# The first chunk of a feed-forward net is normalized beside the last unit of attention

## The reference

```python
x = _layernorm(x + attention(x))          # x is (1, 4096, 256), 16 heads of 16, rotary q and k
x = _layernorm(x + ffn(x))

def ffn(x):                               # 256 -> 1024 -> 1024 -> 1024 -> 256
    h = silu(tlin(x, w1_w, w1_s)) * tlin(x, w2_w, w2_s)
    h = gelu(tlin(h, h1_w, h1_s))         # tlin(x, w, s) = (x @ w.T) * s
    h = gelu(tlin(h, h2_w, h2_s))
    return tlin(h, w3_w, w3_s)
```

## Time and profile before

| | |
|---|---|
| Median of 3 runs | 3526.78 us (3524.37 to 3530.44) |
| Profiled execution, its own time | 3524.76 us |
| Its span (first to last instruction) | 3523.1 us |
| Mean granted clock of TensorE, 1 being full | 0.971 |
| PE busy | 3384.9 us (96%) |
| DVE busy | 2987.0 us (85%) |
| ACT busy | 2451.1 us (70%) |
| POOL busy | 184.7 us (5%) |

### The profile page before, as it was taken

The page is one execution under the profiler, slowest core; times in us unless marked ns, Lnnn a source line. Parts: engine busy times, 40 slices in busy tenths (PEclk is TensorE's granted clock), DMA queues, the critical chain, the costliest instruction groups (busy, mean ns, idle before and its releaser), DMA issues. The chain is left out here.

```text
span 3523.1 us, 67331 instructions
## 1 busy us (share of the span) xinstructions
PE 3384.9 (96%) x27994; PEld 1536.3 (44%) x27994; DVE 2987.0 (85%) x3188; ACT 2451.1 (70%) x4472; POOL 184.7 (5%) x320
## 2 busy tenths in 40 slices
PE   8569999999999999999999999999999699999998
PEld 3223333333333333333333333333333278888887
DVE  6599999999999999999999999999996045555554
ACT  2108888888888888888888888888889622222222
POOL 3300000000000000000000000000000000000000
PEclk9759999999999999999999999999999899999999
DMA  8920000000000010001000000000000220000000
GB/s 212 219 42 6 20 12 12 24 12 12 12 24 16 15 60 14 12 11 61 11 12 30 14 12 12 12 12 12 12 8 5 92 96 25 25 25 26 25 13 13
DMA packets 60037, 113.78 MB, mean 32 GB/s; under 512 B 11719, under 2 KB 23624, under 8 KB 59560
## 3 DMA queue, kind: packets, MB, share of 16 engines
q1 hardware_dynamic: 53048, 93.83, 9.7%
q0 software_dynamic: 6688, 15.68, 1.5%
HBM read 82.20 MB, written 37.22 MB: 34 GB/s over the span
## 5 line engine op out<-in xcount | busy, mean ns | idle before, releaser
L710 DVE TENSOR_REDUCE group_max<-wide 128x2 f32<-128x1024 f32 x2048 | 2473.0, 1223 | 22.5 <-PE wide L521 15.8
L681 ACT ACTIVATE probs<-scores 128x512 f32<-128x512 f32 x4046 | 2202.9, 600 | 290.1 <-PE scores L606 42.0
L547 PE MATMUL sums<-probs,v_all 128*17 128x256 f32 (+1 forms) x16120 | 1277.2, 389 | 7.7 <-ACT mixed L664 6.8
L606 PE MATMUL scores<-q_sb,k_all 51*128 51x512 f32 x3968 | 988.5, 495 | 6.7 <-ACT probs L681 5.7
L521 PE MATMUL wide<-k_all,q_sb 48*128 48x512 f32 x4096 | 850.1, 411 | 52.9 <-DVE group_max L710 26.7
L606 PEld LDWEIGHTS scores<-q_sb,k_all 51*128 51x128 f32 x3968 | 370.6, 183 | 842.9 <-ACT probs L681 829.4
L547 PEld LDWEIGHTS sums<-probs,v_all 128*17 128x17 f32 x16120 | 267.1, 95 | 747.4 <-issue 364.9
L521 PEld LDWEIGHTS wide<-k_all,q_sb 48*128 48x128 f32 x4096 | 397.6, 190 | 91.5 <-DVE group_max L710 63.9
L1073 ACT ACTIVATE whole_hid<-acc,scale 128x512 f32<-128x512 f32 x128 | 84.7, 689 | 297.5 <-PE acc L954 297.3
L954 PE MATMUL acc<-hid_b,h2T 128*128 128x512 f32 x1024 | 241.6, 397 | 0.0
L954 PE MATMUL acc<-hid_a,h1T 128*128 128x512 f32 x1024 | 240.2, 394 | 0.0
(11 more groups left out here) (88 smaller groups left out, 1171.1 us busy)
## 6 DMA issues: line engine op xcount, KB each, us to landing
k_all<-k_parts SPq DMA_DIRECT2D x96, 128.0 KB, 5.2
q_sb<-q_parts SPq DMA_DIRECT2D x192, 64.0 KB, 2.5
q_parts<-parts SPq DMA_DIRECT2D x16, 512.0 KB, 6.0
k_parts<-parts SPq DMA_DIRECT2D x16, 512.0 KB, 6.3
heads<-mixed SPq DMA_DIRECT2D x128, 34.0 KB
xt<-in_xT SPq DMA_DIRECT2D x8, 512.0 KB, 6.3
w_words<-in_h1T POOLq DMA_DIRECT2D x32, 128.0 KB, 2.4
w_words<-in_h2T POOLq DMA_DIRECT2D x32, 128.0 KB, 2.3
```

The costliest lines, as they stand in the source:

```text
L547: last = pe.matmul(sums[32 * j:32 * j + HD + 1, cols], v_all[:, g, kt, j], probs[(kt * HG + j) % RING][:, cols], start=(kt == 0 and cols.s ...
L606: pe.matmul(scores[(s + e) % BANKS][:], k_all[rows, g * GP + j, n // HG * P:(n // HG + 1) * P], q_sb[g][rows, j], start=True, stop=True).t ...
L681: act.activation(probs[n % RING][:], bank, ACT.Exp, scale=INV_SCALE)\
L710: dve.reduce_max(group_max[:, n], wide[n % 2][:], AX_X).then_inc(wide_free, 1)
```

## The change

`attend` now also computes the front of chunk 0. A new class `FirstChunk` lays its tiles, and those of w1T, w2T and h1T, over the place of `k_all` for groups 0 and 1 (what is loaded) and group 2 (x1, x1t, statistics). SP issues the loads after the stores of unit 29 (`load_first`), and the exchange of the inverted sums ahead of the stores of unit 30 (`share_first`). PE has fixed places for its part in the last unit (`beside_last`), where the unread pair of products stands otherwise; ACT takes the square root ahead of the first tile of step 18; DVE does its part after its last maxima. SP no longer waits for the last unit's stores at the block's end: they count on `last_stored`, for which SP and POOL wait in `feed_forward`. There SP first issues h2T and w3T, then the loads of chunk 1; DVE adds, with nine more counts, to the semaphores what the front of chunk 0 would have added, and PE begins with the flag, the branch and `gate_layer(0)`.

```diff
+EARLY_W = ("w1T", "w2T", "h1T")
+            def load_first():
+                for p in range(2):
+                    sp.wait_ge(mixed_free[p], 16 * HG * 3)
+                load_sums(sp, heads_dram, fc.inverse_sums, 0, sums0_in)
+                load_heads(sp, heads_dram, fc.heads, 0, heads0_in)
+                sp.dma_start(fc.x[:], chunk_of(io["x"], 0)).then_inc(x0_in, 16)
+                sp.dma_start(fc.wo[:], io["woT"].rearrange("(f p) o -> p f o", p=P)).then_inc(small0_in, 16)
...
+                sp.wait_ge(w_copied, 16 * len(W_AT))
+                for name in EARLY_W:
+                    load_weights(sp, w_dram, fc.w[name], name, w0_in)
+            def share_first():
+                sp.wait_ge(inverted0, 1)
+                store_inverse(sp, shares_dram, fc.inverse_sums, 0, inverse0_out)
+                sp.wait_ge(inverse0_out, 16)
+                for f in range(FT):
+                    load_shares(sp, shares_dram, fc.shares, 0, f, shares0_in[f])
             for g in range(NG):
                 if g < NG - 1:
                     place_shift((NCH - 1) * NG + g + 1, g + 1)
-                finish(NCH - 1, g)
+                if g == NG - 2:
+                    share_first()
+                finish(NCH - 1, g, mixed_free[g % 2] if g < NG - 1 else last_stored)
+                if g == 1:
+                    load_first()
             for p in range(2):
-                sp.wait_ge(mixed_free[p], 16 * HG * (1 + UNITS // 2))
-            sp.wait_ge(w_copied, 16 * len(W_AT))
+                sp.wait_ge(mixed_free[p], 16 * HG * (1 + UNITS // 2 - p))
+            sp.wait_ge(w0_in, 16 * len(EARLY_W))
+            sp.wait_ge(small0_in, 16 * SMALL)
...
+        BITS_AT, TOK_AT, ROOT_AT, FLIP_AT, SPLIT_BY = 4, 10, 18, 21, 26
+            def beside_last(g, kt):
+                if kt == BITS_AT:
+                    pe.wait_ge(low_done, 1)
+                    pe.wait_ge(ident_set, 3)
+                    pe.matmul(wide[1][0:1, 0, 0:1], low_bits[:], ones[:], start=True, stop=True).then_inc(bits0_summed, 1)
+                elif TOK_AT <= kt < TOK_AT + TT:
+                    tok_first(kt - TOK_AT)
+                elif FLIP_AT <= kt < FLIP_AT + FT:
+                    flip_first(kt - FLIP_AT)
+                elif kt < BITS_AT or BITS_AT + 3 <= kt < TOK_AT:
+                    if kt == BITS_AT + 3:
+                        pe.wait_ge(flag0_set, 1)
+                    unread_pair(g)
+                elif ROOT_AT - 1 <= kt < FLIP_AT:
+                    pe.wait_ge(norm0, TT)
+                    unread_pair(g)
+                elif kt >= SPLIT_BY:
+                    pe.wait_ge(x1t0_step, 2 * FT)
+                    unread_pair(g)
...
+                    if last and n == ROOT_AT * HG:
+                        act.wait_ge(norm0, 3 * TT + 1)
+                        act.activation(fc.root[:], fc.spread[:], ACT.Sqrt).then_inc(root0_done, 1)
...
+            for name in w_in:
+                load_weights(sp, w_dram, w_sb[name], name, w_in[name])
+            load_chunk(1)
+            sp.wait_ge(last_stored, 16 * HG)
...
-            pe.wait_ge(ident_set, 3)
-            pe.matmul(flip[0][0:1, 0:1], low_bits[:], ones[:], start=True, stop=True).then_inc(bits_summed, 1)
-            pe.wait_ge(small_in, 16 * SMALL)
-            front(0)
-            pe.wait_ge(flag_set, 1)
-            front_flip(0, 0)
             low = pe.value_load(flag[0:1, 0:1], min_val=0, max_val=1)
...
-            act.wait_ge(small_in, 16 * SMALL)
-            front_root(0)
             gates(0)
...
+            dve.sem_inc(divided, FT)
+            dve.sem_inc(inverted, 1)
...
+            dve.sem_inc(x1t_step, 2 * FT)
             gates(0)
```

More of the change, by code:

```diff
@@ L358, in attend @@
         probs = [sb(f"probs{r}", [P, CH]) for r in range(RING)]
-        mixed = [sb(f"mixed{p}", [P, CH]) for p in range(2)]
-        ident = sb("ident", [P, P])
+        ones = sb("ones", [P, 1])
         group_max = sb("group_max", [P, MAXG, PAIR])
@@ L570, in last_unit @@
                         if j == 0:
[L572 to L575, removed]
+                            beside_last(g, kt)
                     if kt > 0:
@@ new lines, in _ @@
+            dve.tensor_scalar(fc.flag[:, 0:1], wide[1][0:1, 0, 0:1], 1.0, None, ALU.min).then_inc(flag0_set, 1)
+            dve.wait_ge(heads0_in, FT * 16)
+            for f in range(FT):
+                dve.wait_ge(shares0_in[f], 16)
+                dve.tensor_tensor(fc.heads[:, f], fc.heads[:, f], fc.shares[f][:], ALU.mult).then_inc(divided0, 1)
+            dve.wait_ge(x0_in, 16)
+            for t in range(TT):
+                if t % 2 == 0:
+                    dve.wait_ge(tok0_ready, t // 2 + 1)
+                dve.tensor_tensor(fc.x1[:, t], tok[t // 2][:, t % 2], fc.x[:, t], ALU.add).then_inc(norm0, 1)
@@ new lines, in _ @@
+            for t in range(TT):
+                dve.wait_ge(norm0, t + 1)
+                dve.bn_stats(fc.stats[:, t], fc.x1[:, t]).then_inc(norm0, 1)
+            for t in range(TT):
+                dve.wait_ge(norm0, TT + t + 1)
+                dve.sem_inc(waited0, 1)
+                dve.bn_aggr(fc.moments[:, t], fc.stats[:, t]).then_inc(norm0, 1)
+            dve.wait_ge(norm0, 3 * TT)
+            dve.tensor_scalar(fc.spread[:], fc.moments[:, :, 1], EPS, None, ALU.add).then_inc(norm0, 1)
@@ L754, in sem @@
             return ctx.enter_context(nc.semaphore(name))
[L756 to L770, removed]
-        hid_a = [sb(f"hid_a{h}", [P, HT, CH], F32R) for h in range(2)]
+        fc = first_chunk
+        hid_a = [sb(f"hid_a{h}", [P, HT, CH], F32R) for h in range(2)]
+        sb("before_first_chunk", [P, (fc.at - nc.sbuf_base) // 4])
+        sb("first_chunk", [P, (fc.end - fc.at) // 4])
+        wo, heads, shares, inverse_sums, x_sb, x1t = fc.wo, fc.heads, fc.shares, fc.inverse_sums, fc.x, fc.x1t
+        scale, scale3, flag = fc.scale, fc.scale3, fc.flag
+        w_sb = dict(fc.w)
+        for name, (_, rows, cols) in W_AT.items():
+            if name not in w_sb:
+                w_sb[name] = sb(name, [P, rows // P, cols])
+        x1 = [fc.x1, sb("x1_1", [P, TT, D])]
         hid_b = [sb(f"hid_b{h}", [P, HT, CH], F32R) for h in range(2)]
@@ L817, in feed_forward, with load_chunk @@
         HIDS = 3 * HT
-        SUM_COLS = H * CH // P
-        HF = H // FT
         NORM1 = 4 * TT + 2
         NORM2 = 5 * TT + 2
-        SMALL = 1 + 4 + 1
         EARLY = 3
         block = ctx.enter_context(nc.Block())
[L829 to L841, removed]
         @block.sync
         def _(sp):
[L845 to L850, removed]
+            def load_chunk(c):
+                load_heads(sp, heads_dram, heads, c, heads_in)
+                sp.dma_start(x_sb[:], chunk_of(io["x"], c)).then_inc(x_in, 16)
             def store(c):
@@ L1026, in step @@
                         gate_layer(c + 1)
-                for name in ("w1T", "w2T"):
-                    pe.wait_ge(w_in[name], 16)
                 gate_layer(0)
-                for name in ("h1T", "h2T", "w3T"):
+                for name in w_in:
                     pe.wait_ge(w_in[name], 16)
```

206 lines of the change are left out of this document (142 added, 64 removed).

## The result

The changed kernel takes 3484.08 us, median of 4 runs (3482.10 to 3487.24), beside 3526.82 us (3524.37 to 3530.44) for the kernel before: a ratio of 0.9885, 95% interval 0.9872 to 0.9897. That is 42.7 us less. Forecast were 31.3 us less, 3495.5, range 3489 to 3504. In two experiments one execution each (4910 and 3940 us) is left out of the numbers as disturbed.

The account below looks back on a forecast made before the run. VectorE bounds most of attention, untouched; ACT paces the last unit, and the passage is a chain with nothing beside it. Terms: -31.8 - 6.6 + 2.9 + 1.0 + 2.0 + 1.6 - 0.4 + 0 = -31.3 us, median 3495.5, range 3489 to 3504.

Parts of the forecast that it names:

- (a): Passage: the front of chunk 0, from the net's start to the first gate product, goes; 31.8 us less.
- (b): Passage: SP's wait for the last stores at the block's end goes; 6.6 us less.
- (g): Net's start: eleven semaphore counts on DVE, then PE's flag and branch; 1.6 us more, up to 3.9.
- (c): Last unit, ACT: two table loads, the square root and overlap lost once; 2.9 us more.
- (e): Last unit: PE's clock falls once after idling during the table loads; 2.0 us more, bounds 0 and 3.1.
- (d): Last unit, PE steps 10 to 13: products with wo replace unread pairs, partly absorbed by PE's lead; 1.0 us more.
- (f): Last unit: PE's fixed slots never wait for their producers; 0 us.
- (h): First gate layer: a slightly less slow start after shorter idling; 0.4 us less than the present 17.8.
- (i): First hidden layer: h2T and w3T land at most 18.2 us after the net's start, before needed; 0 us.
- Rival 1: Block's end: the barrier still waits for the last stores through outstanding DMAs; 3502 us, chance 0.08.
- Rivals 2 and 4: Last unit: clock falls several times, 3502 us, chance 0.10; or falls at step 5 and stays low, 3540, chance 0.02.
- Rival 3: Net's start: two late weights come later than a gate layer, branch could need 2.3 more; 3498 to 3501, chance 0.06.

Follow-up runs that it names:

- after_mix2: Changed kernel with x1t, hid_a and hid_b moved 128, 1024 and 512 bytes further from their weights (modulo 2048); 3485.56 us, one execution.
- after_tok8: Changed kernel with its eight products with wo one to a step over steps 7 to 14, not two over 10 to 13; 3489.12 us.
- after_best: Changed kernel with the inverse root on DVE and PE's wait for h2T and w3T after the first hidden layer; 3477.61 us.
- before_free_end: Kernel before with only the wait for the last stores moved out of the block's end into the net; 3520.64 us beside 3525.95.
- before_nopair: Kernel before with the unread pair of products left out of all 32 steps of the last unit; 3520.93 us, one execution.
- after_best2: As after_best, with all unread pairs of the last unit left out too; 3476.39 us, median of three.

## Why the prediction was wrong

By its own steps:

- **The parts behind the first gate layer** were costed at nothing, silently. The steps priced every instruction moved, added or removed, and took those left alone to keep their durations. That is the step that failed: the diff gives the net's tiles other places in SBUF, the distance of moving operand and weights went from -64 to 0 bytes, and the 2496 wide products behind the first gate layer got 16.2 us shorter together (6.7 ns each in the hidden layers, start to start); the eight layers with w3T, where w3T is the moving operand and went from +64 to +256 of hid_a, take 7.92 us instead of 7.78 and give 1.1 back. The stretch as a whole is 15.2 us shorter, and the same got from the kernel before by a pad alone. Without it the result would be about 3484.1 + 15.2 = 3499, inside the range and above the forecast of 3495.5 by the other misses below. The trace before could hardly show it, since all products there went at one pace; a look at the places would have raised the question, but not given the sign.
- **(a), (b), (g)**, the passage: -37.1 against -36.8. Right, and PE takes the branch within the 1.3 us from SP's first issue to its own first product. The upper bound of 3.9 us for a branch that stalls did not come.
- **(c)** 3.1 against 2.9, right. **(e)** one fall behind one gap, as forecast, at 1.2 us against 2.0. But "expect the clock to fall once" is no certainty: it did not in after_mix2, and cost 2.6 in after_tok8.
- **(d)** right in that PE is late in its four steps, wrong in the lead and in the size: 4.2 us net (4.7, less 0.5) against 1.0. Four parts were off: a step of PE without its slot takes 1.84 us and not 1.58 (1.0 us over four steps), the two products hold PE for 1.06 and not 0.86 (0.8), the lead of 0.9 us does not exist, and the transposes, costed at 0, take 0.9. The 1.58 came from rows of another unit at half clock, halved.
- **(f)** right: no slot's producer was late. Ahead of the slot at 2736.32 PE shows no idle by DVE, and h1T was on its way from 2651.62 and took 18.7 us.
- **(h)** 17.4 us for the gate layer once nothing waits behind it, as forecast, with luck: the same layer takes 16.3 to 17.8 in the four kernels of before, and 16.2 in after_best, with the stretches of low clock. **(i)** wrong by 2.2 us: landing was costed at 18.2 us after the start and came 20.9 after it. The last unit's stores, and chunk 1's loads, share the DMA engines; how much each adds was not taken apart.

Rival 1 (the barrier waits for open DMAs) is refuted by before_free_end. The range's low end, 3489, is 1 us under what its own bounds give, 3490; that changes nothing here. Rivals 2 and 4 (the clock falls in steps without a pair) are refuted by the changed kernel and, with no pair at all, by before_nopair and after_best2. Rival 3 came half true, in its weights and not in its branch. The misses of (d) and (i), 3.2 + 2.2 = 5.4 us too little, would have moved the sum toward the range's upper half; they hid a third of the effect that was missed. Of the signs named ahead, one of being wrong came (PE waits for a DMA ahead of the first hidden layer), and the last unit is 8.5 us longer where 4 to 6 were named.

What stays open is why a distance costs. The runs show the dependence on where moving operand and weights start, and that its sign differs between 512 and 256 columns, not what the two operands meet in.

## What to carry to other kernels

When a change moves or adds tiles, compute where the operands of the most frequent instruction land before and after, and do not take its pace for given; no table of distances carries over to another shape, but an experiment of one unused allocation settles it. In a loop where two engines run in lockstep over a few buffers, an engine's idle share is no lead: add up the starts of its instructions over one step, at the clock and in the order of that loop, and expect what exceeds the step to be late. Put a wait for a transfer in front of its first reader, and a rare function that needs another table on an engine that does not need one.

## What the runs showed of the hardware that was not expected

- A product of 128x128 weights with 512 moving columns goes at 226.7 to 233.4 ns by the distance in SBUF alone, 3%, with weights and moving operand both moved together making no difference. One with 256 moving columns (w3T) goes at 118.7 to 121.2 ns, and distance 0 is its slowest.
- Behind a like gap of 2.37 us the clock came back after 3.4 us in the changed kernel and after 6.8 in after_tok8, and in after_mix2 it did not fall.
- A small load took 6.66 us behind four small stores in flight, and 2.67 us when they had landed. In the changed kernel the like load behind the stores of unit 29 took 7.0.
- A full-array product among products of 51 or 17 rows and columns costs more than its own pace: the four records of a step took 1.06 us where the earlier trace rows give 0.86, and two took 0.63 where they give 0.43.
